# Row and column attention: Q and K in 32-half records, V and residual tiles inside them

## What is computed

```python
Q = (x @ Wq).reshape(B, R, C, H, D) * scaling * sw
K = (x @ Wk).reshape(B, R, C, H, D)
V = (x @ Wv).reshape(B, R, C, H, D)
QK = jnp.einsum('brihd,brjhd->bhij', Q, K)
attn = jax.nn.softmax(QK, axis=-1)          # masks left out here
out = jnp.einsum('bhij,brjhd->brihd', attn, V)
return x + out
```

## Time and profile before

| what | value |
|---|---|
| time, median of 3 runs | 654.88 us (654.37 to 658.42) |
| the profiled execution, its own time | 661.25 us |
| its span, which the trace covers | 659.4 us |
| PE busy | 520.1 us, 79% |
| DVE busy | 435.9 us, 66% |
| ACT busy | 253.2 us, 38% |
| POOL busy | 226.1 us, 34% |
| moved by DMA | 152.82 MB, mean 232 GB/s |

### The profile page before, as it was taken

The page is one execution under the profiler, slowest core; times in us unless marked ns, Lnnn a source line. Parts: engine busy times, 40 slices in busy tenths (PEclk is TensorE's granted clock), DMA queues, the critical chain, the costliest instruction groups (busy, mean ns, idle before and its releaser), DMA issues.

```text
span 659.4 us, 14354 instructions
## 1 busy us (share of the span) xinstructions
PE 520.1 (79%) x4984; PEld 427.6 (65%) x4984; DVE 435.9 (66%) x981; ACT 253.2 (38%) x555; POOL 226.1 (34%) x231
## 2 busy tenths in 40 slices
PE   0040399898449999999998999946799989999960
PEld 0030188897335666665667998836799989998850
DVE  3899847899907666666664668803677772668840
ACT  0030246688116555555552114411455550114320
POOL 1010123588204333333331004804466660005840
PEclk9995557899569999999999999989699997999985
DMA  8992005689957879889998999999877722999999
GB/s 281 412 434 93 0 21 162 179 229 249 255 156 206 265 223 261 229 250 233 236 211 219 317 269 292 250 275 283 250 239 239 241 83 93 300 254 272 272 280 254
DMA packets 207258, 152.82 MB, mean 232 GB/s; under 512 B 170032, under 2 KB 190064, under 8 KB 206448
## 3 DMA queue, kind: packets, MB, share of 16 engines
q1 hardware_dynamic: 204960, 151.02, 81.5%
q10 hardware_dynamic: 2256, 1.23, 0.7%
HBM read 95.60 MB, written 56.62 MB: 231 GB/s over the span
## 4 chain that ended last, share of the span: by engine, by line
PE 64%; DVE 15%; DMA 6%; SPq 5%; POOL 3%; issue 2%; ACTq 1%; ACT 1%; POOLq 0%; DVEq 0%
PE PS L1023 9%; PE PS L992 7%; PE PS L993 7%; PE PS L994 7%; PE PS L995 7%; PE PS L996 7%; DVE EXTRA L599 6%; DMA BIG<-in_x 4%; DVE EXTRA L705 3%; PE PS L1052 3%; PE PS L1054 2%; PE PS L1053 2%; PE PS L1055 2%; PE PS L1056 2%; DVE BIG L693 2%; PE PS L871 2%
## 5 line engine op out<-in xcount | busy, mean ns | idle before, releaser
L462 POOL TENSOR_TENSOR BIG<-EXTRA,BIG 128x192 f32 (+1 forms) x144 | 106.5, 740 | 168.3 <-ACT BIG L532 168.3
L766 DVE TENSOR_TENSOR EXTRA<-PS,SW 128x192 f32<-128x192 f32 (+1 forms) x144 | 73.2, 508 | 96.2 <-ACT BIG L546 95.8
L992 PE MATMUL PS<-WP,EXTRA 128*128 128x384 f16 (+1 forms) x384 | 111.1, 289 | 22.1 <-DMA EXTRA<-xt_scratch 12.4
L993 PE MATMUL PS<-WP,EXTRA 128*128 128x384 f16 (+1 forms) x384 | 111.2, 290 | 0.0
L994 PE MATMUL PS<-WP,EXTRA 128*128 128x384 f16 (+1 forms) x384 | 111.1, 289 | 0.0
L995 PE MATMUL PS<-WP,EXTRA 128*128 128x384 f16 (+1 forms) x384 | 111.0, 289 | 0.0
L996 PE MATMUL PS<-WP,EXTRA 128*128 128x384 f16 (+1 forms) x384 | 110.9, 289 | 0.0
L470 POOL TENSOR_TENSOR BIG<-BIG,EXTRA 64x512 f32<-64x512 f32 x42 | 53.2, 1266 | 139.3 <-DVE BIG L838 138.0
L1023 PE MATMUL PS<-BIG,EXTRA 128*128 128x256 f16 x768 | 89.1, 279 | 13.0 <-DVE BIG L838 11.1
L1023 PEld LDWEIGHTS PS<-BIG,EXTRA 128*128 128x128 f16 x768 | 76.1, 100 | 25.2 <-issue 14.1
L453 POOL TENSOR_TENSOR BIG<-EXTRA,BIG 128x1024 f16<-128x1024 f32 x24 | 53.0, 2211 | 74.0 <-ACT BIG L503 73.8
(11 more groups left out here) (155 smaller groups left out, 916.3 us busy)
## 6 DMA issues: line engine op xcount, KB each, us to landing
EXTRA<-xt_scratch SPq DMA_DIRECT2D x48, 512.0 KB, 3.7
BIG<-in_x SPq DMA_DIRECT2D x6, 3072.0 KB, 21.2
EXTRA<-xt_scratch SPq DMA_DIRECT2D x48, 256.0 KB, 3.9
v_scratch<-EXTRA SPq DMA_DIRECT2D x32, 384.0 KB, 4.2
BIG<-v_scratch SPq DMA_DIRECT2D x16, 768.0 KB, 6.7
BIG<-in_x SPq DMA_DIRECT2D x14, 768.0 KB, 9.5
out_x<-BIG SPq DMA_DIRECT2D x14, 768.0 KB, 7.0
xt_scratch<-BIG SPq DMA_DIRECT2D x12, 512.0 KB, 3.3
```

Source lines behind the costliest of these rows:

```text
L462: pool.tensor_tensor(QA[:, :, bass.ds(SI[h] * n + low, SI[h])], TQ[h][g % 4], QA[:, :, bass.ds(SI[h] * n, SI[h])], ALU.subtract).then_inc( ...
L766: v.tensor_tensor(TQ[h][g % 4].rearrange("p (m d) i -> p m d i", d=D), ps[:, :, 0:EH].rearrange("p i (m d) -> p m d i", d=D), swv.unsqueez ...
L992: mm(po, xh0, WP[:, 0, 0, wc], start=True, stop=False)
L993: mm(po, xh0, WP[:, 1, 0, wc], start=False, stop=False)
```

## The change

Q and K of a head now share one region of `BIG`: `[partition, head k, 2C columns, 32 halves]`, where the first 192 column places are highs and the last 192 lows, and a record of 32 halves holds 16 of Q and 16 of K. An operand of a logits matmul, for one d, therefore takes one half from each record: its elements lie 64 bytes apart. V of a chunk lies in the records of columns 0 to 95 (highs and lows), the residual in those of columns 96 to 191. Residual chunks 6 and 7 have places of their own in `EXTRA`; chunk 7 lies over XT 2 and 3. `EXTRA` grows by 1792 words per partition.

```diff
-        QA = BIG[:, 0:AR].bitcast(fp16).rearrange("p (m s) -> p m s", s=2 * C)
-        KA = BIG[:, AR:2 * AR].bitcast(fp16).rearrange("p (m s) -> p m s", s=2 * C)
+        REC = 2 * D
+        HEADW = 2 * C * REC // 2
+        QK = BIG[:, :].bitcast(fp16).rearrange("p (k n f) -> p k n f", k=HALF, f=REC)
+        QA, KA = QK[:, :, :, 0:D], QK[:, :, :, D:REC]
...
-        X_AT = [0, 1, 2, 3, 4, 5, 0, 6]
+        X_AT = list(range(NRC))
...
-            for b in range(4):
-                if b == 2:
-                    for k in range(2):
-                        sp.wait_ge(s_vs[k], V_STORED)
-                load_xt(1, b // 2, b % 2, b)
+            for b in range(2):
+                load_xt(1, 0, b, b)
+            for k in range(2):
+                sp.wait_ge(s_vs[k], V_STORED)
...
             for h in range(2):
                 if h:
+                    for k in (6, 7):
+                        sp.wait_ge(s_out[k], 32)
+                    for b in range(2, 4):
+                        load_xt(1, b // 2, b % 2, b)
                     with sp.Fori(1, TURNS[1]) as t:
...
-                    sp.wait_ge(s_out[X_AT[7]], 32)
+                    sp.wait_ge(s_pj[1], NG[1])
+                load_x(h, 6)
+                load_x(h, 7)
                 for n in range(NV):
                     sp.wait_ge(s_qk[h], n + 1)
                     load_v(h, n)
                     load_x(h, n)
-                load_x(h, 7)
                 for n in range(NRC):
...
                     store_out(h, n)
-                    if n == 1:
-                        sp.wait_ge(s_out[0], 32 * fill(X_AT, h, 0))
-                        load_x(h, 6)
```

ACT's wait for the stores moves from before its first write of pass 1 to turn 3 of 6 (after 96 columns), and DVE's wait for the last low part is gone. The writes of Q and K go in runs of 16 halves to records 64 bytes apart, where before they went in runs of 2 or 4; the product with `SW` keeps one weight for 16 elements in a row, where before it stepped to another column's weight (48 bytes on) at every element:

```diff
-                        v.tensor_tensor(TQ[h][g % 4].rearrange("p (m d) i -> p m d i", d=D),
-                                        ps[:, :, 0:EH].rearrange("p i (m d) -> p m d i", d=D),
-                                        swv.unsqueeze(2).to_broadcast([P, HALF, D, si]),
+                        v.tensor_tensor(TQ[h][g % 4], ps[:, :, 0:EH].rearrange("p i (k d) -> p i k d", d=D),
+                                        swv.unsqueeze(3).to_broadcast([P, si, HALF, D]),
```

The stationary of the other 64 query columns is now highs 128 to 191 and the lows of the first 64 columns, and the last one lows 64 to 191, so low products for the first 64 query columns land beside those of the rest and are added afterwards. The number of matmuls and their moving columns stay:

```diff
-                        mm(p0, QA[:, m, 0:P], kh, start=first, stop=False)
-                        mm(p0, QA[:, m, 0:P], kl, start=False, stop=False)
-                        mm(p0, QA[:, m, 2 * P:3 * P], kh, start=False, stop=last)
-                        mm(p1, QA[:, m, P:2 * P], kh, start=first, stop=False)
-                        ins = mm(p1, QA[:, m, P:2 * P], kl, start=False, stop=last)
+                        q0, q1, q2 = (QA[:, k, t * P:(t + 1) * P, d] for t in range(3))
+                        kh, kl = KA[:, k, 0:C, d], KA[:, k, C:2 * C, d]
+                        mm(p0, q0, kh, start=first, stop=False, skip_group_check=True)
+                        mm(p0, q0, kl, start=False, stop=last, skip_group_check=True)
+                        mm(p1, q1, kh, start=first, stop=False, skip_group_check=True)
+                        mm(p1, q1, kl, start=False, stop=last, skip_group_check=True)
+                        ins = mm(p2, q2, kh, start=False, stop=last, skip_group_check=True)
```

For each head ACT copies 64x384 and 64x192 instead of one 64x192, and DVE does two additions (128x192, 64x192) and one product of 128x384 instead of a product of 128x192, an addition of 64x192 and a product of 64x192:

```diff
-                    nc.scalar.copy(LLOW[k % 2][0:E1, :], PS[E1:P, 2 * (k % 2) + 1, 0:C]).then_inc(s_ll[h], 1)
+                    low = PS[:, 2 * (k % 2) + 1, :].rearrange("p (t n) -> p t n", t=2)[:, :, 0:C]
+                    nc.scalar.copy(LLOW[k % 2][0:E1, :, :], low[E1:P])
+                    nc.scalar.copy(LLOW[k % 2][E1:P, 0, :], low[0:E1, 1, :]).then_inc(s_ll[h], 1)
...
-                    v.scalar_tensor_tensor(lg[:, 0, 0:C], PS[:, 2 * (k % 2), 0:C], alpha, M01[:, 0, :],
-                                           ALU.mult, ALU.mult)
                     dve.wait_ge(s_ll[h], k + 1)
+                    v.tensor_tensor(lg[:, 0, 0:C], PS[:, 2 * (k % 2), 0:C], LLOW[k % 2][:, 0, :], ALU.add)
```

More of the change, by code:

```diff
@@ L64, in row_column_attention @@
         X = BIG[:, :]
-        AR = C * E // 2
-        QA = BIG[:, 0:AR].bitcast(fp16).rearrange("p (m s) -> p m s", s=2 * C)
-        KA = BIG[:, AR:2 * AR].bitcast(fp16).rearrange("p (m s) -> p m s", s=2 * C)
+        REC = 2 * D
+        HEADW = 2 * C * REC // 2
+        QK = BIG[:, :].bitcast(fp16).rearrange("p (k n f) -> p k n f", k=HALF, f=REC)
+        QA, KA = QK[:, :, :, 0:D], QK[:, :, :, D:REC]
         TT = [BIG[:, c * CI * E:(c + 1) * CI * E].bitcast(fp16).rearrange("p (s t n) -> p t s n", t=3, s=2)
               for c in range(NCH)]
-        HW = D * C
-        V0 = [BIG[:, k * HW:k * HW + RI * EH].bitcast(fp16).rearrange("p (r s e) -> p r s e", s=2, e=EH)
+        HW = HEADW // 2
+        V0 = [BIG[:, k * HEADW:k * HEADW + RI * EH].bitcast(fp16).rearrange("p (r s e) -> p r s e", s=2, e=EH)
               for k in range(NV)]
-        V1 = [BIG[:, k * HW + RI * EH:k * HW + RI * EH * 3 // 2].bitcast(fp16)
+        V1 = [BIG[:, k * HEADW + HW:k * HEADW + HW + RI * EH // 2].bitcast(fp16)
               .rearrange("p (r e) -> p r e", e=EH) for k in range(NV)]
-        XO = [BIG[:, AR + k * HW:AR + (k + 1) * HW] for k in range(HALF)]
-        EXTRA = sb("EXTRA", [P, 13056])
+        XO = [BIG[:, k * HEADW:(k + 1) * HEADW].rearrange("p (t a n) -> p t a n", t=2, a=2)[:, :, 1, :]
+              for k in range(HALF)]
+        EXTRA = sb("EXTRA", [P, 14848])
         place = [0]
@@ L103, in row_column_attention @@
         FLAT = part(C * H)
-        at_tq = place[0]
+        at_lg = place[0]
+        place[0] += 2 * 512 + 4 * C
         TQ = [part(4 * EH) for _ in range(4)]
-        TQ = [[q[:, 0:SI[h] * EH].rearrange("p (m i) -> p m i", i=SI[h]) for q in TQ] for h in range(2)]
+        TQ = [[q[:, 0:SI[h] * EH].rearrange("p (i k d) -> p i k d", i=SI[h], d=D) for q in TQ] for h in range(2)]
+        XO = XO + [part(HW).rearrange("p (t n) -> p t n", t=2), EXTRA[:, HW:2 * HW].rearrange("p (t n) -> p t n", t=2)]
+        XO = [q.rearrange("p t (r e) -> p t r e", e=EH) for q in XO]
         AT = [EXTRA[:, o:o + HALF * 2 * C].bitcast(fp16).rearrange("p (h t n) -> p h t n", h=HALF, t=2)
               for o in (at_first, 0)]
-        place[0] = at_tq
+        place[0] = at_lg
         LG = [part(2 * 256).rearrange("p (t n) -> p t n", t=2) for _ in range(2)]
[L113 to L117, removed]
+        LLOW = [part(2 * C).rearrange("p (t n) -> p t n", t=2) for _ in range(2)]
+        OLOW = [EXTRA[:, at_lg + k * 512:at_lg + (k + 1) * 512] for k in range(3)]
         SW = sb("SW", [P, C * H])
@@ L226, in row_column_attention @@
         s_vl = [sem(f"v_loaded{k}") for k in range(NV)]
-        s_xl = [sem(f"residual_loaded{k}") for k in range(HALF + 1)]
+        s_xl = [sem(f"residual_loaded{k}") for k in range(NRC)]
         s_av = [sem(f"attended_psum{h}") for h in range(2)]
@@ L231, in row_column_attention @@
         s_lo = [sem(f"low_part_added{h}") for h in range(2)]
-        s_out = [sem(f"out_stored{k}") for k in range(HALF + 1)]
+        s_out = [sem(f"out_stored{k}") for k in range(NRC)]
         def when(eng, s, value):
@@ L428, in _ @@
                     store_out(h, n)
-                    if n == 1:
-                        sp.wait_ge(s_out[0], 32 * fill(X_AT, h, 0))
-                        load_x(h, 6)
-            for k in range(HALF + 1):
-                sp.wait_ge(s_out[k], 32 * 2 * X_AT.count(k))
+            for k in range(NRC):
+                sp.wait_ge(s_out[k], 64)
         @block.gpsimd
@@ L456, in _ @@
             for h in range(2):
[L457 to L464, removed]
+                with pool.Fori(0, TURNS[h]) as t:
+                    for g in range(SPT[h]):
+                        n = SPT[h] * t + g
+                        pool.wait_ge(s_qh[h], n + 1)
+                        pool.tensor_tensor(QA[:, :, bass.ds(SI[h] * n + C, SI[h]), :],
+                                           TQ[h][g % 4].rearrange("p i k d -> p k i d"),
+                                           QA[:, :, bass.ds(SI[h] * n, SI[h]), :],
+                                           ALU.subtract).then_inc(s_ql[h], 1)
                 for j, (n, hp) in enumerate(BLOCK):
@@ L531, in q_high @@
                     act.wait_ge(s_tq[h], n + 1)
[L532 removed]
+                    nc.scalar.copy(QA[:, :, bass.ds(SI[h] * n, SI[h]), :],
+                                   TQ[h][g % 4].rearrange("p i k d -> p k i d")).then_inc(s_qh[h], 1)
                 def body(t, late=False):
@@ L545, in body @@
                                            ).then_inc(s_kvh[h], 1)
-                        nc.scalar.copy(KA[:, :, bass.ds(SI[h] * n, SI[h])],
-                                       ps[:, :, EH:2 * EH].rearrange("p i m -> p m i")).then_inc(s_kvh[h], 1)
+                        nc.scalar.copy(KA[:, :, bass.ds(SI[h] * n, SI[h]), :],
+                                       ps[:, :, EH:2 * EH].rearrange("p i (k d) -> p k i d", d=D)
+                                       ).then_inc(s_kvh[h], 1)
                         if g or not isinstance(t, int):
                             q_high(n - 1, g - 1)
-                if h:
```

(10 more changed lines are left out.)

15 lines of the change are left out of this document (6 added, 9 removed).

## The result

The changed kernel takes 872.32 us (median of 4, 871.04 to 873.28), the kernel before 655.57 us beside it. The ratio is 1.330, with a 95% interval of 1.325 to 1.335. The profiled execution's span is 869.3 us against 659.4.

The account below looks back on a forecast made before the run. It took passes to end when their bytes are through; stepped logits matmuls at 160 ns make PE pace: heads of 13.7 us, span 706.2 against 659.4, 46.8 us more on the 654.9 median: 701 us, range 641 to 725.

Parts of the forecast that it names:

- Rival 3: Logits matmuls: each far element costs PE what it costs DVE, 1.74 ns; spacing 334 ns, 868 us; chance 9%.
- Stationary operands: no term.: Logits' stationary loads, 25 ns each, could become three times as long before showing under 83 ns; nothing added.
- (a): Pass 0's value transfers: XT 2 and 3 leave the queue, 4.1 us, so the last store lands at 460.2.
- (b): Hand-over between passes: XT 2 and 3 load after the last store, 5.2 us; PE resumes at 465.4, not 466.27.
- (c): Pass 1: residuals 7 and 6 leave the full queue for the projection's end; gain 9.6 us.
- (d): Writes of Q and K: DVE's SW product loses its extra 0.26 us, hidden beside PE; at most 0.26 us per pass.
- (e): Two larger copies and additions per head, some 0.5 us on ACT and 0.2 on DVE: hidden; PE might wait 1 us.
- The rest of the sum: Whole span apart from the head's price: end = 351.0 + 12 x head + 52.3 + 84.2 + 54.3.
- The threshold of 111 ns: Logits matmul spacing up to which the change does not lose: a head of 9.8 us, 1.34 times the present spacing.
- The slope of 0.96 us per ns: Beyond 111 ns, each further ns of logits matmul spacing costs 0.96 us of the whole time.

Follow-up runs that it names:

- e3: Kernel before, with the logits' moving operand read in another step or run for each head; 82.5 to 346 ns a matmul, no total time given.
- e2: Changed kernel, with only the logits' moving operands read in a row and the stationary ones still stepped; 651.18 us, 82.5 ns between matmuls.
- e4: Kernel before, with the logits' stationary operand stepped 2 to 64 bytes, in pass 1 with 24 moving columns; 26.7 to 62 ns a load.
- e5: Kernel before, with pass 1's residual chunk 7 loaded ahead of its XT loads and chunk 6 at the projection's end; 652.81 us, ratio 0.995.
- e1: Changed kernel, with both operands of the logits read in a row instead of 64 bytes apart; 650.67 us, ratio 0.990 to the kernel before.
- e7: Changed kernel, with the logits' moving halves read 8 bytes apart instead of 64; 725.0 us, span 723.2 us.
- e9: As e6, but pass 1's turn 1 XT loads go first and residual chunk 7 follows in four pieces; 640.55 us, ratio 0.976.
- e6: As e5, and pass 0's residual chunk 7 is loaded two rows at a time during its projection; 647.83 us, ratio 0.989.

## Why the prediction was wrong

**The direction was right, the size was not.** I forecast 701 us and a range of 641 to 725; it is 872. The term that failed is s, the spacing of the logits' matmuls. Its bounds, 83 and 334 ns, were drawn from the rows and the truth lay inside, at 323.3, hard by the upper one. I then took 160, "nearest to the ratio" of DVE's stepped to its plain price. Rows 8 had the figure in it: 1.74 ns for each weight read 48 bytes on. e3 gives 1.7 to 1.8 ns for each 16-byte piece on PE. So it behaves as a time for a piece, not as a factor on the reader's own rate; that DVE's and PE's price have one cause is argued from the like figures, not shown. PE, whose columns take 0.43 ns each, loses nearly a factor of four where DVE, at 1.06 ns an element, lost 1.64. Rival 3 said this and came to 868 us; I gave it 9% with the argument that a memory "would have to fall to a quarter", and it does.

**What made me discard the row** was pass 0's form, two weights in turn without a price, which I called a sign that the row was not clean. The changed kernel's row for pass 1 points to the weights' step: 558 ns once the weight stands still for 16 elements. The read of `PS` came into order too, but the low half of K read it in the same steps at 552 ns before and takes 548 in order, so that part has no price. Why two weights in turn cost nothing was not tried and stays open.

**The page's rule.** The Trainium skill (SBUF — State Buffer, "SBUF: two separate sides") asks for two accesses to a 16-byte line to reach full rate. The size of the line agrees: 16, 32 and 64 bytes apart cost about the same, 8 bytes half. The two accesses are not enough for this moving operand: the 8-byte step has two and takes 172 ns against 82.5. The measurement decides.

**"Stationary operands: no term."** Right for this kernel: 62 ns at most, hidden (e2, e4).

**"(a) the last store would land at 460.2" and "(b) PE could resume at 465.4".** Wrong, and by the reading of a row. The store that lands at 464.27 is chunk 6's, for which ACT waited, since only the six places in `BIG` held it up. Chunk 7's store, out of `EXTRA`, was issued at 460.45 and 461.40 us (first line, the kernel before). In e5, whose pass 0 is as before, its second part is issued at 460.89 and stands in the chain (second line):

```profile
461.40 3.72 SPq L408 DMA_DIRECT2D out_x<-EXTRA  x1
...
460.89 6.95 DMA out_x<-EXTRA
```

So the pass before ended near 468, an estimate, and not at 464. With XT 2 and 3 behind the last store, e1's ends at 462.4: the queue did gain, but the new wait is for a later store than the old one. The hand-over costs 2.8 us more instead of 0.9 less.

**(c)** Right in kind, with some 7.5 us by the medians of e1 (11.4 between the two traces) for 9.6. **(d)** Right: DVE's and POOL's gains are there and move nothing; ACT's copies keep their time (479 ns for 384 elements, before 478). **(e)** Right: in e1 PE waits 0.20 us before the sixth head's transposes, under full transfers.

**The rest of the sum** held to within about 1 us of span at two spacings (e7 and the changed kernel); the way from span to median did not (e7), and 701.7 rounds to 702. In the changed kernel its errors nearly cancel: from the end of the heads (350.07 + 6 x 27.2 = 513.3) to pass 0's last store at 568.6 it is 55.3 us for 52.3: V 6 goes out after 10.8 us for 9.6, and from there it is 44.5 us for 42.7, a term that rests on the misread store; but XT takes 4.7 us for 5.2, the way from there to pass 1's logits (573.27 to 651.29) 78.0 for 79.0, and the logits of pass 0 begin 0.9 us earlier. The threshold of 111 ns was not tried; e2 at 82.5 ns and e7 at 177 ns lie on either side. The slope of 0.96 us per ns is 1.00 between e7 and the changed kernel (869.3 - 723.2 = 146.1 us for 146.4 ns).

## What to carry to other kernels

- For a matmul's moving operand count the 16-byte pieces it touches, not its columns alone: here each took 1.7 to 1.8 ns, so that four halves used out of every piece kept 192 columns within 3% of 82.5 ns, and two did not. A stepped stationary operand took at most 62 ns for 128 columns, which a matmul of 192 columns hid.
- When a price is known for one engine, ask whether it is a time or a factor before carrying it over: by a time of 1.74 ns DVE lost a factor of 1.64 and PE nearly four.
- In a stretch bound by its bytes, look for the hole before it: three residual chunks moved into the projections, one in pass 0 and two in pass 1, gave 2.4% (e9), and their place in the queue decided whether it came through (e5, e6). And name the very store that a wait is for.

## Not expected of the hardware

- The price came out alike on DVE (1.74 ns a weight, in pass 1's form alone) and PE (1.68 to 1.80 ns a piece), and on PE at either level of its granted clock: the changed kernel's matmuls stand some 320 ns apart at 1.00 (351 us) and 323 ns apart at 0.50.
- PE was busy for all of 360 to 380 us, with 63 matmuls, and its granted clock was 0.50: a PE held up by its operand reads ran at the lower level. Held up less, at 177 ns in e7, it kept 1.00 (380 to 420 us). After the logits the attended values began at that lower level: the first 48 matmuls of pass 0 took 7.39 us, against 5.35 us in the kernel before.
